# First-layer batches of a two-layer cross-attention kernel: values directly behind the scores, both side steps behind them

## What is computed

```python
# layer 0 attention (heads of 8, temporal bias), then layer 1 attention
scores = jnp.einsum('bhqd,bhkd->bhqk', q, k) * SCALE
scores = scores + _temporal_bias(L_q, L_kv)[None, None, :, :]
attn = jax.nn.softmax(scores, axis=-1)
attended = jnp.einsum('bhqk,bhkd->bhqd', attn, v)
...
x = x + _L0_xattn_ref(_layernorm(x, axis=-1), ctx_1024, ...)
x = x + _L0_ffn_ref(_layernorm(x, axis=-1), ...)
x = x + _L1_xattn_ref(_layernorm(x, axis=-1), ctx_1024, ctx_1024, mask, ...)
x = x + _L1_ffn_ref(_layernorm(x, axis=-1), ...)
```

## Time and profile before

| | us |
|---|---|
| median of 3 runs | 569.89 |
| lowest and highest of these | 567.97, 572.94 |
| the profiled execution, whole | 571.24 |
| its span, first to last instruction | 567.8 |
| PE busy in the span | 505.2 (89%) |
| ACT busy | 433.0 (76%) |
| DVE busy | 280.4 (49%) |
| POOL busy | 171.2 (30%) |

### The profile page before, as it was taken

One profiled execution on the slowest core, in us unless ns is written; L12 is line 12 of the kernel. 1 busy time (PEld: TensorE's weight loads), 2 busy tenths in 40 slices (PEclk: granted clock), 3 DMA queues, 4 the chain that ended last, 5 costly groups with the idle time before them and its releaser, 6 DMA issues.

```text
span 567.8 us, 15324 instructions
## 1 busy us (share of the span) xinstructions
PE 505.2 (89%) x6318; PEld 256.2 (45%) x6318; DVE 280.4 (49%) x741; ACT 433.0 (76%) x493; POOL 171.2 (30%) x207
## 2 busy tenths in 40 slices
PE   7677798899889998999999999899989999998994
PEld 4344454445444554455555444444444444343332
DVE  4853665774586455654523252325434543261156
ACT  1235587677768787687898999899988998899841
POOL 4464945486488124871001000100000000000003
PEclk9897999999999999999999999999999999999998
DMA  8575884579557802575184356229411840000000
GB/s 264 157 231 161 258 289 112 158 223 306 142 161 214 304 16 75 166 218 163 27 178 141 110 123 158 60 46 202 119 55 47 178 145 2 12 1 1 8 6 15
DMA packets 51583, 74.52 MB, mean 131 GB/s; under 512 B 11146, under 2 KB 40050, under 8 KB 51506
## 3 DMA queue, kind: packets, MB, share of 16 engines
q1 hardware_dynamic: 40258, 37.54, 26.4%
q0 software_dynamic: 5632, 24.07, 12.9%
q10 hardware_dynamic: 5616, 11.86, 6.7%
HBM read 39.95 MB, written 18.83 MB: 104 GB/s over the span
## 4 chain that ended last, share of the span: by engine, by line
PE 60%; ACT 15%; issue 10%; DVE 8%; POOL 4%; DMA 2%; ACTq 0%; DVEq 0%; POOLq 0%
PE ps L538 26%; PE ps L514 16%; ACT probs L1173 9%; PE ps L449 4%; PE ps L439 2%; PE ps L668 2%; ACT ctx_turned L1173 2%; DVE k_swapped L1473 1%; PE ps L443 1%; ACT ctx_tokens L1173 1%; DMA k_scratch<-k_parts 1%; ACT k_parts L1198 1%; PE ps L702 1%; PE ps L550 1%; PE ps L519 1%
## 5 line engine op out<-in xcount | busy, mean ns | idle before, releaser
L1173 ACT ACTIVATE probs<-ps 124x1024 f32<-124x1024 f32 (+1 forms) x305 | 296.2, 1025 | 56.1 <-PE ps L519 44.6
L514 PE MATMUL ps<-q_side,k_side 64*124 64x256 bf16 (+1 forms) x1664 | 161.9, 290 | 38.3 <-ACT probs L1173 30.1
L538 PE MATMUL ps<-probs,values 124*9 124x256 f32 (+1 forms) x2440 | 162.8, 382 | 0.0
L514 PEld LDWEIGHTS ps<-q_side,k_side 64*124 64x124 bf16 (+1 forms) x1664 | 79.4, 130 | 144.9 <-ACT probs L1173 77.4
L538 PEld LDWEIGHTS ps<-probs,values 124*9 124x9 f32 (+1 forms) x2440 | 52.7, 90 | 63.5 <-issue 16.7
L1043 POOL TENSOR_TENSOR post_rstd<-post_rstd,power 128x2 f32<-128x2 f32 x12 | 8.4, 703 | 194.2 <-DVE post_rstd L1688 126.7
L519 PE MATMUL ps<-bias_near,bias_w 64*124 64x84 bf16 (+1 forms) x416 | 42.2, 200 | 0.0
L1173 ACT ACTIVATE ctx_tokens<-ps 124x1024 f32<-124x1024 f32 (+1 forms) x37 | 38.0, 1026 | 4.9 <-PE ps L514 4.0
L1473 DVE SCALAR_TENSOR_TENSOR k_swapped<-ps,beta_products,k_table_sb 32x496 f32<-32x496 f32 (+2 forms) x64 | 40.4, 632 | 0.9
L1173 ACT ACTIVATE ctx_turned<-ps 124x1024 f32<-124x1024 f32 (+1 forms) x37 | 37.9, 1025 | 3.4 <-PE ps L514 2.4
L1173 ACT ACTIVATE ctx_normed<-ps 124x1024 f32<-124x1024 f32 (+1 forms) x37 | 37.9, 1025 | 2.4 <-PE ps L514 1.6
(11 more groups left out here) (250 smaller groups left out, 634.7 us busy)
## 6 DMA issues: line engine op xcount, KB each, us to landing
k_side<-k_scratch SPq DMA_DIRECT2D x24, 400.2 KB, 7.8
k_scratch<-k_parts POOLq DMA_DIRECT2D x16, 372.0 KB, 4.9
k_side<-k_parts SPq DMA_DIRECT2D x45, 124.0 KB, 2.4
q_side<-q_parts SPq DMA_DIRECT2D x63, 64.0 KB, 2.5
v_scratch<-values POOLq DMA_DIRECT2D x4, 936.0 KB, 9.9
values<-v_scratch SPq DMA_DIRECT2D x4, 936.0 KB, 14.3
v_scratch<-v POOLq DMA_DIRECT2D x12, 288.0 KB, 4.7
mask_q<-in_mask POOLq DMA_DIRECT2D x8, 400.5 KB, 4.2
```

Source lines behind the costliest of these rows:

```text
L514: last = pe.matmul(ps[0:width, bank, SQ * i:SQ * (i + 1)], kst[rows, j % 2, 2 * g + i, at], qst[rows, query_slot(j, run), 2 * g + i, :], s ...
L538: last = pe.matmul(ps[32 * i:32 * i + VC, ACC + g // 2, SQ * (g % 2):SQ * (g % 2) + SQ], v[0:rows, j % 2, t, h, :], probs_of(u)[0:rows, SQ ...
L1173: act.activation(probs_of(u)[0:rows, :], ps[0:rows, s:s + 2, :].rearrange("p a n -> p (a n)"), ACT.Exp)\
```

## The change

In the passes before `WIDE_FROM` (j = 0, 1, 2) the side step of the even slot no longer stands between the scores and the values of its gap, but behind the values, directly ahead of the side step of the odd slot. From pass 3 on the order is as before. No instruction is added or removed, and the other engines' programs are the same.

```diff
-                beside(j, 2 * pair)
+                if j >= WIDE_FROM:
+                    beside(j, 2 * pair)
                 for i in range(values_at(j, pair)):
                     values(taken)
                     taken += 1
+                if j < WIDE_FROM:
+                    beside(j, 2 * pair)
                 beside(j, 2 * pair + 1)
```

## The result

| | us |
|---|---|
| before, median of 4 runs (lowest, highest) | 570.45 (567.97, 572.94) |
| after, median of 4 runs (lowest, highest) | 583.67 (583.5, 584.68) |
| ratio after / before, 95% interval | 1.0234 [1.0205, 1.0262] |
| the profiled execution of after, whole | 583.5 |
| its span | 581.2 |

The change makes the kernel slower by 13.2 us, or 2.3%. The forecast was 578.0, in a range of 572 to 583, so the direction was right and the time lies 0.7 us above the range.

What follows compares the result with a forecast made beforehand. The prediction took the loop of scores, exponential and scores two units later as the bound. Its terms, 6.9 + 0.5 + 0.7 + 0.3 - 0.5 = 7.9 us, gave 577.8 from the median, predicted as 578, range 572 to 583.

Steps and rivals of the forecast that it cites:

- The loop: Passes 0 to 2: scores, exponential, scores two units later bound the time, through the exponential held behind second_keys.
- Keys steps: Eleven keys steps at even slots of passes 0 to 2, each 0.98 us later: together 6.9 us.
- The full ones: Keys steps at slots 24, 28, 40 of pass 0, 14 of pass 1, 18 of pass 2: 0.98 us each, uncovered.
- the ones with a filled wait: Slot 46 of pass 0 and 26 of pass 1: values fill PE's wait for DVE, leaving 0.73 and 0.36 us.
- Slot 20 of pass 1: Keys step: a filled wait leaves 0.51 us, absorbed five slots later by PE's 0.80 wait for DVE; cost 0.
- Slot 8 of pass 0: Keys step: ACT's 1.39 us wait for POOL exceeds the delay; cost 0.
- Slot 2: Keys step of pass 0: second_keys waits 6.65 us for a transfer there; cost 0.
- Pairs, queries, gates: Dependent pairs in one gap: fold_weights 0.5, centre_x and sample 0.7 us; later query parts 0.3; gates' filled waits -0.5.
- The clock: No loss taken for 2.1 us stalls; rival: 2.3 us per drop, two giving 582.4, nine 598; chance 0.09.
- Its own sign of being wrong: The forecast is wrong if the granted clock falls under 1.00 between 82 and 285 us.
- Absorbed: Rival: ACT's waits behind keys steps take up the delay; half gives 574.4, four fifths 572.3; chance 0.17.
- The filled waits: Rival: held exponential off the path, so only PE's filled waits, 2.3 us less 1.2 for pairs, count: 568.8; chance 0.08.

Runs made afterwards that it cites:

- e11: Before, with ACT's second_keys of an even keys step also waiting for the next gap's first scores; PE's order untouched: 588.96 us, ratio 1.032.
- e4: After, with ACT's second_keys of an even slot s moved behind exp(s + 3) instead of exp(s + 2): 568.25 us, ratio 0.9962 to before.
- e6: Before, with ACT's second_keys of an even slot s moved behind exp(s + 3) instead of exp(s + 2): 563.98 us, ratio 0.988.
- e2: After, with the eleven even keys steps put back ahead of the values, other even side steps still behind them: 571.07 us, ratio 1.0021 to before.
- e8: After, plus four matmuls of zeros in the gap behind each even keys step, ahead of the stalling scores: 578.28 us, ratio 1.0147 to before.
- e1: After, plus nine matmuls of zeros in the gap behind each even keys step, ahead of the stalling scores: 580.11 us, ratio 1.0151 to before.
- e12: Before, with second_keys of an even slot s behind exp(s + 3), the same kernel as e6 timed again: 565.28 us, ratio 0.9911.
- e9: e6 plus six matmuls of zeros in the gap three further on than the keys step, same pass only: 569.28 us, ratio 0.9976 to before.

## Why the prediction was right and wrong

**The loop.** Right. The held exponential behind `second_keys` was on the path: e11 made it later without the change and cost 19 us, e4 and e6 took it off and the order hardly mattered any more. The 1.14 us stall of the earlier trace rows was the sign to read, since it showed that nothing else covered that loop.

**Keys steps.** Right in nearly every term. The full ones cost 0.98 to 1.02 against 0.98, the ones with a filled wait 0.70 and 0.31 against 0.73 and 0.36. Slot 20 of pass 1 was absorbed by DVE's wait five slots later, as said. Slot 8 of pass 0 was taken at 0 and came to 0: the values filled a wait of PE for DVE there (0.31), and ACT's wait for POOL shrank from 1.39 to 0.72 and took up the other 0.67. Slot 2 was taken at 0 too; the 0.51 found there came with the transfer, at a place that e2 shows to vary without the change.

**Pairs, queries, gates.** 0.43 and 0.58 for 0.5 and 0.7; -0.54 for -0.5. PE's waits appear where they were forecast: 0.64 at L575 (0.7 forecast) and 1.70 at L472 (0.87 in the earlier trace rows). The query parts cost 0.04 instead of 0.3: their delay came (0.37) and was absorbed again (0.33). Together with the keys steps the sum was 7.9; with the clock held it was 7.89 in passes 0 to 2 (e8) and 8.1 by the medians. Some 0.5 of that is the transfer at slot 2, so the terms of the order alone were about 0.5 too high, and the closer agreement is luck.

**The clock: the step that failed.** "No row shows a stall of 2.1 us. I take no loss, as 2.1 is nearer to 1.3." Its own sign of being wrong came up: the granted clock is 0.96 from 82 to 290. The value chosen was the wrong end of a bound between 1.3 (no drop) and 6.23 (a drop). The lower end was even a little lower than the text says: the longest stall of before between 82 and 277 is 1.14, and its 1.31 ended at 65.41. Here five of eight stalls of 1.91 to 2.12 us brought the clock to 1.2 GHz, and these cost 6.9 us in passes 0 to 2 and 5.4 by the medians. The sum's 7.9 and this make about the 13.2. The Trainium skill (TensorE: Matmul & The Clock Gate, Part 1) says that the slow clock is the default and that activity lifts it. The runs agree: e1 and e8 put activity into the stall, changed little else, and had a granted clock of 1.00 from 60 to 280 where after had 0.96.

**Its price.** A drop was put at 2.3 us, from the one at 45. Each measured 1.33 to 1.58. The 2.3 took the values, the side step and the scores all at the slow clock. But each drop lasted 3.4 to 3.5 us and covered one of them only in part: at 158.73 the side step lost 0.36 instead of 0.9 (1.49 against 1.13), and at 92.80 the values lost 0.37 (1.42 against 1.05). Two drops gave 582.4 in the rival, nine 598. Five of them at 1.5, less 0.66 absorbed, on top of 577.8 give 584.7; measured 583.67. The rival had the mechanism, its chance of 0.09 was far too small, and the range, which held only two drops, was too narrow at its upper end.

**The other rivals.** Absorbed: it happened at slots 8 of pass 0 and 20 of pass 1 and with the queries, 0.66 of the clock's loss too, but not in general. The filled waits are all there, at about the forecast size, and are outweighed.

**What stays open.** Why the stalls that ended at 57.30, 115.27 and 183.93 in after brought no drop, and a shorter one of 1.69 in e6 did; and why e12 had a drop that the same kernel in e6 had not. Why `mask_q` came later in e1 and e9 than in the others. e4 and e6, alike from unit 20 on, differ by some 3.3 us ahead of it. Their waits for the transfer at slot 2 differ (5.51 and 3.97), and so do those of e6 and e12, the same kernel (3.97 and 4.30, with 1.65 us between them by unit 20). So at least a part of the 3.3 is not the order; how much isn't shown.

## What to carry to other kernels

Before a producer is moved later, look at what is queued behind its reader on the reader's engine. If the product's consumer holds back an instruction of the main loop and no other wait takes up the delay, it is paid in full at every such step. Here moving the consumer in its own queue was worth more than either order of the producer. A PE stall that grows towards 2 us in an otherwise busy stretch has to be costed with a lost clock as well, at its likely number of times.

## What the runs showed of the hardware

- TensorE's granted clock fell from 2.4 to 1.2 GHz behind stalls much shorter than the 6.23 us of the earlier trace rows. Followed by a drop: five of eight of 1.91 to 2.12 us in after, six of eight of 2.23 to 2.44 in e11, one of 2.02 in e4 and one in e6, one of 1.69 in e6, one of 1.82 in e12, one of 2.42 in e1. Not followed: three of 1.91 to 1.93 in after, two of 2.23 and 2.25 in e11, one of 2.00 in e4, one of 1.81 in e6, those of 1.31 and the one of 1.70 (L472) in after, and all eight of 1.37 to 1.58 behind zeros in e8. So length alone doesn't decide in this range, and two executions of one kernel (e6, e12) can differ.
- A drop cost this kernel 1.33 to 1.58 us. Where they fell wholly into one, a gap's values took 1.90 instead of 1.05 and its scores 0.68 instead of 0.43.
- Four matmuls of zeros with 9 columns, three of which took 0.49 us, put ahead of each of these stalls, were enough to keep the clock at 1.00 from 60 to 280 in e8, with up to 1.58 us of the stall left bare. Nine (e1) did no more.
